# A transformer block on one core: experts' first products three tiles ahead, biases folded into the split weights, second-stage weights loaded in pieces

## What is computed

```python
x = x + _L0_attn_a_ref(_layernorm(x), ...)   # 16 heads of 64, ALiBi, causal, softmax, output product, bias
x = x + _L0_ffn_ref(_layernorm(x), ...)      # experts
x = x + _L0_attn_b_ref(_layernorm(x), ...)   # 8 heads of 128, rotary, causal, softmax
x = x + _L0_ffn_ref(_layernorm(x), ...)      # experts again, same weights
```

```python
h = x * rsqrt(mean(x * x) + eps) * norm_w
logits = h @ gate_w.T + gate_b               # 8 experts
vals, idx = top_k(logits, 2); wts = softmax(vals)
t1 = einsum('td,efd->tef', h, mlp1_w) + mlp1_b
act = swiglu(t1)                             # min(glu, 7) * sigmoid(1.702 glu) * (clip(lin) + 1)
y = einsum('tei,edi->ted', act, mlp2_w) + mlp2_b
out = sum of the two chosen y, weighted; returns x + out
```

## Time and profile before

| | us |
|---|---|
| median of 3 runs (lowest, highest) | 2245.36 (2244.46, 2257.79) |
| the profiled execution | 2245.2 |
| its span, first to last instruction | 2243.4 |
| TensorE busy | 2116.7 (94%) |
| VectorE, ScalarE, GpSimd busy | 1531.3, 1442.4, 1288.7 |

### The profile page before, as it was taken

How to read it: one execution, slowest core, us unless ns; L and a number is a source line. 1 busy time by engine, 2 the same in 40 slices (tenths; PEclk the granted TensorE clock), 3 DMA queues, 4 the chain that set the end, 5 groups by cost and what they waited for, 6 DMA issues and landing times.

```text
span 2243.4 us, 38399 instructions
## 1 busy us (share of the span) xinstructions
PE 2116.7 (94%) x11652; PEld 1710.4 (76%) x11652; DVE 1531.3 (68%) x4349; ACT 1442.4 (64%) x3737; POOL 1288.7 (57%) x1458
## 2 busy tenths in 40 slices
PE   7999999999999999899997999999999999899992
PEld 5677777777777777678876788788888888677782
DVE  7768686868686858367766667566675666556665
ACT  5868686868686867444444778667776576634443
POOL 4755555555555545467654647566666656466661
PEclk9999999999999999999998999999999999999996
DMA  3320000000000000434331101001010000522426
GB/s 130 132 85 29 1 29 1 29 1 29 1 29 1 20 1 28 167 97 103 112 126 54 38 10 39 29 20 48 11 38 29 1 20 13 212 76 76 161 88 244
DMA packets 55140, 132.34 MB, mean 59 GB/s; under 512 B 12256, under 2 KB 30208, under 8 KB 53920
## 3 DMA queue, kind: packets, MB, share of 16 engines
q1 hardware_dynamic: 37216, 92.58, 11.2%
q0 software_dynamic: 17728, 37.32, 6.1%
HBM read 81.51 MB, written 48.35 MB: 58 GB/s over the span
## 4 chain that ended last, share of the span: by engine, by line
PE 77%; DVE 7%; ACT 6%; issue 4%; POOL 3%; DMA 2%; another core or an unknown queue 0%; SPq 0%; DVEq 0%; ACTq 0%; POOLq 0%
PE bank L621 6%; PE bank L1431 5%; PE bank L1451 5%; PE bank L643 5%; PE bank L2141 5%; PE bank L603 5%; PE bank L1416 3%; PE bank L588 3%; PE bank L1331 3%; PE bank L2116 3%; PE bank L2115 3%; PE bank L2117 2%; PE bank L589 2%; PE bank L1333 2%; PE bank L1332 2%
## 5 line engine op out<-in xcount | busy, mean ns | idle before, releaser
L1111 POOL TENSOR_TENSOR P<-P,rc 128x128 f32<-128x128 f32 (+3 forms) x512 | 354.3, 723 | 359.1 <-DVE rc L929 358.8
L921 DVE CUSTOM_DVE_ANT_0 P<-bank,tab 128x512 f32<-128x512 f32 (+3 forms) x512 | 240.4, 485 | 117.3 <-PE bank L589 114.9
L765 ACT ACTIVATE P<-P,mn 128x128 f32<-128x128 f32 (+3 forms) x512 | 281.6, 552 | 38.3 <-DVE mn L921 34.0
L776 ACT COPY PT<-bank 128x512 f32<-128x512 f32 (+1 forms) x384 | 194.4, 516 | 98.0 <-PE bank L603 90.7
L1930 POOL TENSOR_TENSOR q<-rf,q 128x512 fp32r<-128x512 f32 x128 | 163.2, 1297 | 135.9 <-ACT q L1553 135.8
L1923 POOL TENSOR_TENSOR rf<-rp 128x512 f32<-128x512 f32 x128 | 163.7, 1279 | 134.6 <-DVE rp L1750 133.1
L603 PE MATMUL bank<-cst,P 128*128 128x128 f32 x1280 | 207.4, 277 | 14.0 <-POOL P L1111 6.8
L2348 POOL DMA_INDIRECT yD<-Yf,place x142 | 138.8, 978 | 131.3 <-ACT Yf L2205 118.7
L2191 ACT ACTIVATE sgf<-glf 128x256 f32<-128x256 f32 x142 | 59.3, 418 | 229.5 <-DVE glf L2262 229.4
L588 PE MATMUL bank<-q 128*128 128x512 f32 (+3 forms) x512 | 185.3, 373 | 10.1 <-DVE mn L921 5.1
L603 PEld LDWEIGHTS bank<-cst,P 128*128 128x128 f32 x1280 | 153.6, 141 | 42.2 <-ACT PT L776 11.5
(11 more groups left out here) (237 smaller groups left out, 5978.2 us busy)
## 6 DMA issues: line engine op xcount, KB each, us to landing
hD<-hh SPq DMA_DIRECT2D x16, 512.0 KB, 2.6
W1lf<-w1lD SPq DMA_DIRECT2D x2, 4096.0 KB, 13.0
yg<-yD SPq DMA_DIRECT2D x14, 512.0 KB, 4.4
X<-in_x SPq DMA_DIRECT2D x8, 512.0 KB, 4.6
stage<-in_w SPq DMA_DIRECT2D x8, 512.0 KB, 3.5
w1hD<-W1A SPq DMA_DIRECT2D x8, 512.0 KB, 2.6
w1lD<-stage SPq DMA_DIRECT2D x8, 512.0 KB, 3.6
rD<-xn SPq DMA_DIRECT2D x8, 512.0 KB, 2.9
```

The lines of the kernel that those rows point to most:

```text
L765: i = e.activation(ps, ps, ACT.Exp, bias=mn[:, pb, t:t + 1], scale=-1.0, accum_out=rs[:, pb, t:t + 1])
L776: e.copy(PT[:, h % 2, PTO[cs[0]]:PTO[cs[0]] + w], bank[4 + n % 2][:, 0:w]).then_inc(q.a_pt, 1)
L921: e.tensor_tensor_reduce(out=P[:, pb, OFF[t]:OFF[t] + w], in0=score(h, t), in1=tab[:, 512 - w:512], scale=-SLOPES[h % 16], scalar=3e38, op ...
L1111: i = e.tensor_tensor(ps, ps, rc[:, h % 3, t:t + 1].broadcast_to([128, w]), ALU.mult)
```

## The change

- **First biases in the split weights.** Feature 0 of the normalised rows is no longer stored: hh's column 0 is set to 1 once, and the normalisation writes columns 1 to 255 (in both attention stages). Since a normalised row sums to zero, feature 0 is minus the sum of the others; so row 0's weights (times norm_w[0]) are subtracted from every row of the first weights and of the gate, and row 0 of the weights in memory is overwritten by the biases. For this `norm_w1` becomes a scalar_tensor_tensor with a second operand, share, loaded per expert by a 256 KB broadcast from a new buffer w0D; the loop stores the high part as soon as it is made; three small copies put the biases into row 0 after the loop. `up` no longer has the bias matmul; BR holds only the second biases.
- **Three tiles ahead in three banks.** `up` uses banks 0, 1 and 6, gl, li, sg and ac have three places, and the order on TensorE is flip_x(a + 4), up(a + 3), flip_a(a + 1), down(a). ScalarE, VectorE and GpSimd follow: gather(a + 7), and put_ids 4 to 7 before the loop.
- **Second stage's weights.** W1l, W2 and W1h are loaded in 17 pieces, each as the buffers under it fall free; the residual store of batch 6 moves in between; the residual's loads xr are spread over the loop.
- **Ranks.** In attention a `top_two` piece 3 and `route` piece 0 move from places 55 and 57 to 53 and 54; in attention b the last batch's rank moves behind the transpositions of its unit.

```diff
                     def gate_logits(bt):
-                            e.wait_ge(v_gw, 1)
+                            e.wait_ge(v_gw, 4)
...
                     high(1, 1)
                     exps(0)
                     exps(1)
-                    e.wait_ge(d_b0, 16)
+                    e.wait_ge(d_b0, 32)
...
+                            else:
+                                e.memset(hh[:, :, 0:1], 1.0)
                         for t in (2 * half, 2 * half + 1):
-                            i = e.tensor_scalar(hh[:, t], X[:, bt % 3, t], mvs[:, 1, t, 0:1], r2[:, t:t + 1], ALU.subtract,
-                                                ALU.mult)
+                            i = e.tensor_scalar(hh[:, t, 1:D], X[:, bt % 3, t, 1:D], mvs[:, 1, t, 0:1], r2[:, t:t + 1],
+                                                ALU.subtract, ALU.mult)
...
-                    def norm_w1(i):
-                        e.wait_ge(d_w1s, 16 * i + 16)
-                        for kc in range(2):
-                            e.tensor_scalar(stage[:, kc], stage[:, kc], nw[:, kc:kc + 1], None, ALU.mult).then_inc(v_w1, 1)
+                    def norm_w1(i, kc):
+                        e.wait_ge(d_w1s, 32 * i + 32)
+                        e.scalar_tensor_tensor(stage[:, kc], stage[:, kc], nw[:, kc:kc + 1], share[:, 0:512], ALU.mult,
+                                               ALU.subtract).then_inc(v_w1, 1)
...
-                            elif at == 55:
+                            elif at == 53:
                                 top_two(e, q, 3, bt - 1, lg, v8, i8, if8, dv)
-                            elif at == 57:
+                            elif at == 54:
                                 route(e, q, 0, bt - 1, 0)
...
                                 e.dma_start(stage[:].rearrange("p a b -> p (a b)"), T["w1"][:, k]).then_inc(d_w1s, 16)
+                                e.dma_start(share[:, 0:512], w0D[k].partition_broadcast(128)).then_inc(d_w1s, 16)
+                                e.wait_ge(p_w1, 2 * i + 1)
+                                e.dma_start(w1hD[:, k], W1h[:, k % W1_STAY].bitcast(F32)).then_inc(d_w1o, 16)
                                 e.wait_ge(p_w1, 2 * i + 2)
-                                e.dma_start(w1hD[:, k], W1h[:, k % W1_STAY].bitcast(F32)).then_inc(d_w1o, 16)
                                 e.dma_start(w1lD[:, k], stage[:].rearrange("p a b -> p (a b)")).then_inc(d_w1o, 16)
...
                             scores(u + 1, 1)
                             scores(u + 1, 0)
                             turn_p(u, 2)
+                            if p == 6 and bt == NB - 1:
+                                e.wait_ge(q.v_lg, bt)
+                                e.wait_ge(r_st, 9)
+                                rank(e, 1, bt - 1)
...
                     def up(a):
-                        k, o = a % 2, bank[a % 2]
+                        k, o = a % 2, up_bank(a)
...
-                        if a > 1:
-                            e.wait_ge(v_gl, 3 * (T0 + a - 2) + 2)
+                        if a > 2:
+                            e.wait_ge(v_gl, 3 * (T0 + a - 3) + 2)
                         r = e.value_load(etab[0:1, a:a + 1], min_val=0, max_val=E - 1)
                         ex = bass.ds(r, 1)
-                        e.matmul(o[:], on[:, a:a + 1].broadcast_to([128, 128]), BR[:, 0:512], start=True, stop=False)
...
                     up(1)
+                    flip_x(2)
                     outproj(BL, 0)
-                    flip_x(2)
+                    up(2)
+                    flip_x(3)
+                    flip_a(0)
                     for a in range(NS):
-                        flip_a(a)
+                        if a + 4 < NS:
+                            flip_x(a + 4)
                         if a + 3 < NS:
-                            flip_x(a + 3)
-                        if a + 2 < NS:
-                            up(a + 2)
+                            up(a + 3)
+                        if a + 1 < NS:
+                            flip_a(a + 1)
                         down(a)
...
+                    x_low(2)
                     residual(BL, 0)
-                    x_low(2)
+                    act(2)
+                    x_low(3)
...
                     gather(e, ph, q, 5)
+                    gather(e, ph, q, 6)
+                    for n in range(4, 8):
+                        put_ids(e, ph, BL - 1, n)
                     for a in range(NS):
-                        if a + 6 < NS:
-                            gather(e, ph, q, a + 6)
-                        if a < 4:
-                            put_ids(e, ph, BL - 1, a + 4)
-                        elif 16 <= a < 28 and a % 3 != 0:
+                        if a + 7 < NS:
+                            gather(e, ph, q, a + 7)
+                        if 16 <= a < 28 and a % 3 != 0:
                             put_ids(e, ph, BL, (a - 16) - (a - 16 + 1) // 3)
...
-                        e.wait_ge(q.m_qk, 2 * NU)
-                        e.dma_start(flat(W1l[:]), w1lD).then_inc(d_w, 16)
-                        e.dma_start(W2[:], T["w2"]).then_inc(d_w2, 16)
+                        e.wait_ge(q.m_v, 8 * NB)
+                        e.dma_start(flat(W1l[:, 2:6:3]), w1lD[:, 2:6:3]).then_inc(d_w, 16)
+                        for x in (0, 6):
+                            e.dma_start(W2[:, x:x + 2], T["w2"][:, x:x + 2]).then_inc(d_w2, 16)
...
                     if last:
-                        fetch_ids(e, ph, 1)
+
+                        e.wait_ge(q.p_xs, NB)
+                        e.wait_ge(q.d_r, 16 * NB)
+                        for bt in range(NB):
+                            if bt == NB // 2:
+                                fetch_ids(e, ph, 1)
+                            e.wait_ge(f_up, T0 + (14 + 3 * bt if bt < NB // 2 else 32 + 4 * bt))
+                            e.dma_start(xr[:, bt], rDv[1][bt]).then_inc(d_xr, 16)
```

138 lines of the change are left out of this document (89 added, 49 removed).

## The result

| | before | after |
|---|---|---|
| median, us | 2246.12 (4 runs, 2244.46 to 2257.79) | 2222.76 (4 runs, 2215.97 to 2225.67) |
| the profiled execution | 2245.2 | 2223.1 |
| its span | 2243.4 | 2221.3 |

The ratio is 0.988 (95% interval 0.984 to 0.992): the change makes the kernel faster by half of what I had forecast, and 2222.8 lies above my range (2188 to 2218).

What follows compares the result with a forecast made beforehand. The prediction took TensorE's own instructions in the expert loops as the bound. Its terms, led by -32.7 us for the bias matmul, summed to -44.6: from 2245.2 to 2200.6 us, range 2188 to 2218.

Steps and rivals of the forecast that it cites:

- What bounds the kernel: Opening step: TensorE holds 77% of the chain, its matmuls follow without idle time, one expert tile takes 3.02 us.
- activation waits: Expert loops: one more tile of cover removes three waits for turned activations inside the loop, -2.8 us.
- residual loads: Second expert stage: issuing the eight loads one by one removes a 2.07 us gather wait and slow clock, -4.0 us.
- put_ids: First expert stage: four list writes leave GpSimd's tiles 0 to 3 and lie under the output projection, -1.5 us.
- GpSimd's own rate: Expert loops, tiles 16 to 27: GpSimd already sets the pace, so the bias matmul's gain there is lost, +5.6 us.
- Starts: Start of both expert stages: TensorE's 0.80 us wait for x_low becomes about twice as long, +1.6 us.
- Ends: End of both expert stages: waits for turned activations and half clock mostly go, 3.0 a stage, -6.0 us.
- First batch: First attention batch: the loop preparing the first weights grows from 12.01 to 12.5 us a round, +3.0 us.
- last rank of the second attention: Last batch's rank, moved behind unit 62's transpositions, saves part of a 2.21 us wait and half clock, -3.8 us.
- Ranks of the first attention: First attention: rank() loses its 0.8 us wait for the routing mask in six batches, -4.0 us.
- Rival 2: Whole kernel: only the matmul counts, the waits removed come back elsewhere, 2221 us; chance 0.12.
- Rival 1: Expert loops: GpSimd takes the bound and never catches up, tiles 16 to 70 keep 3.02, 2220 us; chance 0.12.

Runs made afterwards that it cites:

- bias_only: The kernel before with only the first biases in the split weights and no bias matmul in up, every order as before: 2246.6 us, ratio 0.998.
- combo: pad_vector plus the split behind act(a + 3), tile 3 transposed and split ahead of tile 2's first product, and two small broadcasts later: 2206.5 us, ratio 0.9805.
- pad_vector: The changed kernel with VectorE's clearing of the bias rows cut into 49 pieces, 48 instructions more: 2214.7 us, ratio 0.9843.
- pad_split: pad_vector with VectorE's half of the weight split moved behind act(a + 3): 2289.0 us on the slower kind of chip.
- pad_start: pad_vector with tile 3 transposed and split ahead of the first product of tile 2: 2283.6 us on the slower kind of chip.
- combo_again: combo unaltered, run again on the slower kind of chip: 2276.3 us against 2292.9 for the kernel before, ratio 0.9921.
- changed_again: The changed kernel unaltered, timed again: 2228.5 us against 2249.0 for the kernel before, ratio 0.9907.
- small_loads_late: The changed kernel with the two small broadcasts issued behind the loads of x: 2290.7 us, ratio 0.9964, on the slower kind of chip.

## Why the prediction was wrong

- **What bounds the kernel.** "So in the expert loops TensorE's own instructions are the time, and an instruction less is time less." This is the step that failed, by what it left out. The tile came out at 2.80, but the view that gave me 3.02 was a steady tile of the second stage; in a shorter tile the other engines' work of the tiles that are not steady shows, and the sum had no term for that nor for a stop outside the loops. Over 2.80, tiles 4 to 69 hold 20.5 us in the first stage and 17.2 in the second, where they held 16.3 and 16.6 over 3.02. So 130 x 0.22 = 28.6 was earned and 4.8 given back, where I had counted a further 2.7 as won (activation waits 2.8, residual loads 4.0, put_ids 1.5, less GpSimd's 5.6). bias_only says the same from the other side: 17.4 of 27.1 in the loops.
- **The weight splits** had no term. Eight tiles from 37 on give back 0.5 each, 4 us, and parts of those before. On the first kind of chip combo shows the gain (6.8 in the first stage with the start order, 0.7 in the second with that order alone, so some 6).
- **GpSimd's own rate**: the traces bear the mechanism out, no experiment tested it where the waits are. Its lead is used up at tiles 25 and 99, and the price is not 0.23 a tile but a wait of 2.6 and 3.0 and a tile at half clock behind it. That also took what the residual loads were to give (-4.0).
- **Starts** (-0.2 with their matmuls, +3.4 like for like): the wait for x_low was 1.76, near the 1.6 forecast, and the pause behind it 0.49 instead of 0.40. The rest, 3.3, is the clock of the first stage, half of it ahead of that wait, and it is not there in every execution. **Ends** (-6.9 with their matmuls, -6.5 like for like) were right: the waits of 1.14 and 1.15 are below 0.2 each, and nothing runs at half clock.
- **The stop in the second attention**: 6.2 to 8.0 us on the first kind of chip, over a quarter of the error and the largest single piece. No row of before could show it. It comes with bias_only too, so no order of tiles causes it. 48 VectorE instructions lifted it in pad_vector and combo, but pad_split, pad_start and combo_again have it in spite of them. That the loading of blocks for two engines at once is the cause is not shown, and the traces speak against it: pad_vector loads two such blocks without a stop, and pad_split stops with no block loaded. The cause stays open. The Trainium skill ("Runtime: NRT & Kernel Launch", Instruction fetch mechanics) calls the cost of crossing a block boundary "mostly hidden". Whether this stop of 6.2 us is such a crossing no run here shows.
- **First batch** (+3.0; +2.1 measured in attend(0) to attend(8)), **last rank of the second attention** (-3.8; -3.7) were right.
- **Ranks of the first attention** (-4.0): from attend(8) to the first product it is -4.0, but in part by luck. The six ranks gave 0.37 a batch and not 0.8, -2.2 in all, because from 170 to 925 us 3.4 of the 4.8 of waits for masks came back as waits for maxima; before and after:

```profile
PE bank L588 <- DVE mn L921: 0.7, 2, 0.4
PE bank L593 <- DVE mn L928: 4.1, 9, 0.6
```

  Another 3.7 came at units 60 to 62, where the last batch's rank had waited 1.52 and run on at half clock, which I had not counted, and 1.9 was lost again before the first product (0.1 in changed_again). The +0.6 of this stretch holds a start of the first unit 2.4 later, which small_loads_late found to be scatter.
- **Rivals.** Rival 2 (only the matmul counts, the waits come back elsewhere, 2221) has the number. Its mechanism holds in the loops; that the number fits is in part luck, since the stop of 6.2 is not in it. Without the stop the time would be an estimated 2222.8 - 6.2 = 2216.6, inside my range and still 16 above the forecast. Rival 1's place was right, tiles 16 to 34, but GpSimd did catch up.

Open, beside the stop: what the matmul is worth on the first kind of chip in the new order. The kernel with it never fell there.

## What to carry to other kernels

When the bounding engine's work per tile shrinks by 7%, list for every other engine what it does in a tile that is *not* the steady one (a split, a list write, a normalisation) and hold its chain against the new, shorter tile; that, and not the steady tile, gives the gain. Order such work behind the short links that the bounding engine waits for. And look in the profile of a changed program for stops of two engines that nothing releases: here one cost as much as a part of the change, and a few dozen instructions at an idle place lifted it on one chip, not on every other. Compare like stretches: a median that doesn't move can hide a loss in the loops and a gain of chance elsewhere.

## What the runs showed that I had not expected

- Two engines stop together for 6 to 10 us with their inputs ready, at the same unit in profile after profile. With 48 instructions placed 490 us earlier the time fell from 2228.5 to 2214.7 on one chip, with the run-to-run range down from 6.4 to 1.2; of the eleven profiles with them, five have no stop, three a short one and three nearly all of it.
- The same program takes 2246 to 2249 us on some chips and 2293 to 2299 on others, and a change's ratio goes with it (0.9843 and 0.9951 for pad_vector's kernel). The first difference to see is 17 pauses of ScalarE in the expert loops, 58.7 us in all, that nothing releases.
- With such pauses, 34 us more work on TensorE cost 11 to 16 in the loops and nothing measurable in the whole.
- A wait of 2.2 us at the start of a stage is followed by a granted clock of 0.85 in 19 starts and of 1.00 in 7, with the same instructions; with tile 3 transposed ahead of the first product of tile 2 it was 1.00 in eight of eight. The stage's first tile, ahead of the wait, had 1.00 in some profiles and 0.50 in others.
